# Output projection as seven block products over two query groups, shared products added by VectorE from its banks; first statistics spread by TensorE

## The reference

```python
xn = (x - mean(x)) / sqrt(var(x) + 1e-5)                    # per token
q, k, v = split(xn @ Wqkv + bqkv)                           # one head, d = 512
attn = softmax(q @ k.T / sqrt(512)) @ v                     # 2048 x 2048 per sequence
gate = softmax over the 16 largest of 64 (xn @ Wq_w.T @ keys.T), 0 elsewhere
z = (xn @ A_w.T).reshape(.., 64, 8) * gate                  # 512 columns
out = x + attn @ Wo + bo + (z @ B_w.T) * 2
```

## Time and profile before

| | |
|---|---|
| median of 3 runs | 2846.6 us (2846.41 to 2846.97) |
| profiled execution, its own time | 2843.56 us |
| its span | 2841.0 us |
| TensorE, VectorE, ScalarE, GpSimd busy | 97%, 53%, 30%, 14% of the span |
| matmuls in the trace | 12096 |
| mean over the 16 DMA engines | 224 GB/s |

### The profile page before, as it was taken

The page is one execution under the profiler, slowest core; times in us unless marked ns, Lnnn a source line. Parts: engine busy times, 40 slices in busy tenths (PEclk is TensorE's granted clock), DMA queues, the critical chain, the costliest instruction groups (busy, mean ns, idle before and its releaser), DMA issues.

```text
span 2841.0 us, 33300 instructions
## 1 busy us (share of the span) xinstructions
PE 2749.1 (97%) x12096; PEld 2244.6 (79%) x12096; DVE 1496.1 (53%) x1875; ACT 854.7 (30%) x1146; POOL 389.6 (14%) x293
## 2 busy tenths in 40 slices
PE   6888999999999999999979999999999999999999
PEld 4676878878888888888868788888888888888887
DVE  6665876467745776455574634324444344333431
ACT  3552225622364233322242221111322212112110
POOL 0011000000000000000031504205032050320501
PEclk9999999999999999999989999999999999999999
DMA  7589665455555364324766967758688686775866
GB/s 299 184 300 319 218 209 199 148 163 178 174 200 157 119 216 138 97 97 163 253 244 247 343 226 253 279 203 296 240 275 303 238 287 216 250 281 197 284 233 234
DMA packets 268159, 636.01 MB, mean 224 GB/s; under 512 B 30192, under 2 KB 54896, under 8 KB 263792
## 3 DMA queue, kind: packets, MB, share of 16 engines
q1 hardware_dynamic: 233968, 546.54, 56.2%
...
## 4 chain that ended last, share of the span: by engine, by line
PE 85%; DVE 5%; DMA 4%; ACT 3%; issue 2%; SPq 0%; POOL 0%; ACTq 0%; DVEq 0%; POOLq 0%
PE psum L750 35%; PE psum L1632 15%; PE psum L1634 15%; PE psum L1633 15%; PE psum L687 2%; DMA stat_scratch<-mv 2%; DMA w_raw<-t_scratch 1%; ACT rows L534 1%; DVE prob L1834 1%; DMA w_raw<-W_blocks 1%; DVE r_lo L1806 1%; ACT w_hi L479 1%; DVE w_lo L800 1%; ACT rows L537 1%; PE psum L1755 0%
## 5 line engine op out<-in xcount | busy, mean ns | idle before, releaser
L800 DVE TENSOR_TENSOR w_lo<-w_raw,w_hi 128x1024 fp32r<-128x1024 f32 x224 | 274.2, 1224 | 433.7 <-ACT w_hi L479 433.5
L479 ACT ACTIVATE w_hi<-w_raw 128x1024 fp32r<-128x1024 f32 x224 | 237.5, 1060 | 775.2 <-PE psum L750 677.8
L1632 PE MATMUL psum<-r_hi,f_hi 128*128 128x512 f32 x1024 | 401.9, 392 | 4.6 <-DVE r_lo L1806 3.3
L1634 PE MATMUL psum<-r_hi,f_lo 128*128 128x512 f32 x1024 | 399.2, 390 | 0.0
L1633 PE MATMUL psum<-r_lo,f_hi 128*128 128x512 f32 x1024 | 399.1, 390 | 0.0
L750 PE MATMUL psum<-s_hi,w_hi 128*128 128x512 f32 x896 | 353.7, 395 | 28.1 <-DVE w_lo L800 16.4
L750 PE MATMUL psum<-w_hi,s_hi 128*128 128x512 f32 x896 | 351.4, 392 | 15.9 <-DVE w_lo L800 14.9
L750 PE MATMUL psum<-s_hi,w_lo 128*128 128x512 f32 x896 | 351.3, 392 | 0.0
L750 PE MATMUL psum<-s_lo,w_hi 128*128 128x512 f32 x896 | 351.3, 392 | 0.0
L750 PE MATMUL psum<-w_lo,s_hi 128*128 128x512 f32 x896 | 350.3, 391 | 0.0
L750 PE MATMUL psum<-w_hi,s_lo 128*128 128x512 f32 x896 | 350.2, 391 | 0.0
...
## 6 DMA issues: line engine op xcount, KB each, us to landing
...
w_raw<-t_scratch SPq DMA_DIRECT2D x128, 512.0 KB, 4.0
...
res<-x SPq DMA_DIRECT2D x128, 256.0 KB, 6.1
out<-res SPq DMA_DIRECT2D x128, 256.0 KB, 7.2
...
```

The costliest lines, as they stand in the source:

```text
L479: nc.scalar.activation(w_hi[:, s % RAW], w_raw[:, s % RAW], ACT.Copy).then_inc(s_whi, 1)
L800: nc.vector.tensor_tensor(w_lo[:, s % RAW], w_raw[:, s % RAW], w_hi[:, s % RAW].bitcast(F32), ALU.subtract).then_inc(s_wlo, 1)
L1632: pe.matmul(bank, sh, mh, start=first, stop=False)
L1634: return pe.matmul(bank, sl, mh, start=False, stop=last)
```

## The change

**Output projection.** Two query groups (1024 tokens, rows 1 and 2) and two column halves of 1024 form 2 x 2 blocks: x11, x21 are attn of the two groups, x12, x22 their z; b11, b12 are the halves of Wo, b21, b22 of B_T. An output stage w covers a pair (w // 2) and 512 columns of each half (w % 2), and takes seven products of 512 tokens x 512 columns with an inner size of 512, two items each: 14 items, 336 matmuls. Sums of x blocks (s1 to s4, `sum_x`) and their low parts (`low_x`) are made by VectorE, 128x1024 each; high parts by ScalarE. Sums of weight blocks (t1 to t4) are made once by GpSimd beside S0 to V1 (`sum_weights`, 16 of 128x1024, with 16 loads and 16 stores of 0.5 MB) and kept in `sum_scratch`. A finished product is added from its banks to the one to three quarters of the output that need it (`take_product`, 40 additions a stage), except that products 2, 3 and 6 go on accumulating in a bank of an earlier one (CHAINED). The accumulators `part_out` hold x plus bias; GpSimd's queue loads x in 1 MB quarters (`load_rows`), SP stores quarters of 1 MB (`store`).

Since a pair must be complete first, the order of stages is now S0 S1 V0 V1, then S t, O t-2, V t for t = 2 to 7, then O6 O7, written out without loops. Weights are split in O0 and O1 now. A product's addition trails its last item: two tiles in each of the next two items, and the last product's eight additions stand at the start of the next value stage. The low part of z and attn is made where it is used (`low_x`), not in the value stage.

**First statistics.** For group 0 the second half is spread by TensorE too, behind item 6 of the first product (`spread_own`), without DRAM. VectorE computes two of its four tiles (bn_stats), ScalarE the other two; the rows are loaded early into buffers that are free then. x12's rows come as one transfer of 2 MB by GpSimd's queue, the sums of the second product (MIX0) begin one item earlier, and VectorE takes the first part of product 1's result (`take_first_kq`) instead of ScalarE.

```diff
+MIX0_AT = [(0, 7), (1, 0), (1, 1), (1, 2), (1, 3), (1, 4), (1, 5), (1, 6), (1, 7)]
...
-OWN_AT = {(0, 3): 4, (0, 5): 6, (0, 6): 7}
+OWN_AT = {(0, 0): 4, (0, 2): 6}
...
+    def own_rows(j):
+        source = (rows[:, 1, :], part[:, 1, 0:4, :].rearrange("p a c -> p (a c)"),
+                  part[:, 1, 4:8, :].rearrange("p a c -> p (a c)"), part[:, 2, 0:4, :].rearrange("p a c -> p (a c)"))
+        return source[j - HT]
...
+                    if first and (idx, s) == (0, 7):
+                        for a in range(2):
+                            act.wait_ge(s_spread, 3 + a)
+                            nc.scalar.activation(mean_rstd[:, a, W:TG], psum[:, a, :], ACT.Copy).then_inc(s_stat0, 1)
...
+                    if static(g) and g == 0 and (idx, s) == (0, 6):
+                        spread_own()
...
+        def spread_own():
+            for a in range(2):
+                bank_read(pe, 0, 0, 0, a)
+                pe.wait_ge(s_diag, HT + 2 + a)
+                for j in range(HT):
+                    mm = pe.matmul(psum[:, a, j * P:(j + 1) * P], ones[:],
+                                   part[:, 2, HT + a, j * P:(j + 1) * P], start=True, stop=True)
+                mm.then_inc(s_spread, 1)
...
+            elif block == 1 and static(g) and g == 0:
+                dve.wait_ge(s_x12, 16)
...
+        def take_first_kq(banks):
...
+                nc.vector.scalar_tensor_tensor(part[:, 1, b, :], psum[:, b, :], b_diff[:, b:b + 1],
+                                               part[:, 0, b, :], ALU.add, ALU.add).then_inc(s_evA, 1)
...
-                        if s == 4:
-                            stats_of_tile(HT + 1)
+                        if s in (3, 4):
+                            stats_of_tile(HT + 1 + 2 * (s - 3))
...
+                            rstd_finish(2, (HT + 2) * TILE_STEPS + RSTD_STEPS, slice(HT, NTOK))
+                            dve.wait_ge(s_rstd, 2)
+                            for a in range(2):
+                                nc.vector.tensor_tensor(
+                                    part[:, 2, HT + a, :].rearrange("p (a b) -> p a b", b=P),
+                                    ident[:].unsqueeze(1).to_broadcast([P, HT, P]),
+                                    mv[:, a, HT:NTOK].unsqueeze(2).to_broadcast([P, HT, P]), ALU.mult).then_inc(s_diag, 1)
+                    if first and (idx, s) in MIX0_AT:
+                        step = MIX0_AT.index((idx, s))
...
+        pool.wait_ge(s_tiles, 2)
+        pool.dma_start(xb[:, 1], xT[HK * P:2 * HK * P, 0:W].rearrange("(a p) t -> p a t", p=P)).then_inc(s_x12, 16)
...
+    PRODUCTS = [("x11", "b11"), ("s3", "t3"), ("x12", "b21"), ("x22", "t4"), ("s2", "t2"), ("s4", "b22"), ("s1", "t1")]
+    CHAINED = (2, 3, 6)
...
+    EV = {0: 0, 1: 12, 2: 16, 3: 20, 4: 24, 5: 28, 6: 32}
+    EVS = 40
+    X_SUMS = {"x11": 0, "x12": 0, "x22": 0, "s1": 1, "s2": 2, "s3": 1, "s4": 3}
...
+    STAGES = [("S", 0), ("S", 1), ("V", 0), ("V", 1)]
+    for t in range(2, NQ):
+        STAGES += [("S", t), ("O", t - 2), ("V", t)]
+    STAGES += [("O", NQ - 2), ("O", NQ - 1)]
...
+                if kind == "O":
+                    sp.wait_ge(b_qlo, 2 * (t + 3))
...
+                    if PRODUCTS[i // 2][1][0] == "t":
+                        sp.wait_ge(b_wst, 16 * 16)
...
+        def store(w, c):
+            base, col = out_rows(w, c)
+            sp.wait_ge(b_oev, w * EVS + {C11: EV[3], C21: EV[5], C12: EVS, C22: EVS}[c])
+            sp.dma_start(out[base:base + QG, col:col + W].rearrange("(j p) w -> p j w", p=P),
+                         out_quarter(w, c)).then_inc(b_st[c], 16)
...
+                if i == 10:
+                    store(w, C11)
...
+                        mm = three(psum[:, P_BANK[q][j], :], xh[:, a, tok], xl[:, a, tok], wh[:, cols], wl[:, cols],
+                                   begin and q not in CHAINED, end)
...
+            else:
+                pe.wait_ge(b_oev, (t - 2) * EVS + EV[5] + d + 1)
...
+            b11, b12, b21, b22 = (weight_piece(n) for n in ("b11", "b12", "b21", "b22"))
...
+            pool.wait_ge(b_wld, 16 * 4 * (kt + 1))
+            nc.gpsimd.tensor_tensor(b12, b22, b12, ALU.subtract).then_inc(b_wsum, 1)
+            pool.wait_ge(b_wsum, 4 * kt + 1)
+            nc.gpsimd.tensor_tensor(b11, b12, b11, ALU.add).then_inc(b_wsum, 1)
+            pool.wait_ge(b_wsum, 4 * kt + 2)
+            nc.gpsimd.tensor_tensor(b21, b21, b11, ALU.subtract).then_inc(b_wsum, 1)
+            nc.gpsimd.tensor_tensor(b22, b22, b11, ALU.subtract).then_inc(b_wsum, 1)
...
+        def load_rows(w, c):
...
+            pool.dma_start(out_quarter(w, c),
+                           x[base:base + QG, col:col + W].rearrange("(j p) w -> p j w", p=P)).then_inc(b_x, 16)
...
+            elif t == 1:
...
+            else:
+                for c in (C22, C21, C12, C11):
+                    load_rows(t - 2, c)
+                for c in (C22, C21, C12, C11):
+                    add_bias(t - 2, c)
...
+            if t < NQ:
+                sums(t, range(1, 10))
...
+        def sum_x(w, j):
...
+            if name == "s3":
+                nc.vector.tensor_tensor(low, x11, x21, ALU.subtract).then_inc(b_xsum, 1)
...
+            nc.vector.tensor_tensor(low, x21, x22, ALU.add).then_inc(b_xsum, 1)
+            if steps >= 2:
+                dve.wait_ge(b_xsum, base + 1)
+                nc.vector.tensor_tensor(low, low, x11, ALU.subtract).then_inc(b_xsum, 1)
...
+                dve.wait_ge(b_xsum, base + 2)
+                nc.vector.tensor_tensor(low, x12, low, ALU.subtract).then_inc(b_xsum, 1)
...
+        def low_x(w, j):
...
+            nc.vector.tensor_tensor(lo, source, hi.bitcast(F32), ALU.subtract).then_inc(b_xlo, 1)
...
+        def take_product(w, q, tiles):
...
+            for j in tiles:
+                product_ready(dve, w, q, j)
+                if q == 0:
+                    for c in (C22, C21, C12):
+                        dve.wait_ge(b_xb, 4 * QT * w + (BIAS_ORDER[w].index(c) + 1) * QT)
+                        add_product(w, c, j, BANK_A[j])
...
+                    add_product(w, C12, j, BANK_B[j])
+                else:
+                    dve.wait_ge(b_oev, base + EV[5] + j + 1)
+                    add_product(w, C12, j, BANK_A[j])
+                    add_product(w, C22, j, BANK_A[j])
...
+        def output(w):
+            t = w + 2
+            for i in range(LEN["O"]):
+                split_next("O", w, i)
...
+                if i >= 2 and i // 2 - 1 < NP - 1:
+                    take_product(w, i // 2 - 1, (0, 1) if i % 2 == 0 else (2, 3))
...
+                if i + 2 < LEN["O"]:
+                    low_x(w, i + 2)
...
+                if t < NQ and 3 <= i <= 7:
+                    less_maximum(t, 2 * i - 6)
+                    less_maximum(t, 2 * i - 5)
+                if i + 3 < LEN["O"]:
+                    sum_x(w, i + 3)
...
+                if t < NQ and i == LEN["O"] - 1:
+                    low_probability(t, 0)
+                    low_probability(t, 1)
...
+                if t >= 2 and i == 0:
+                    take_product(t - 2, NP - 1, range(QT))
...
+                if i <= 2 and t != 1:
+                    less_maximum(t, 10 + 2 * i)
+                    less_maximum(t, 11 + 2 * i)
...
+        stages({"S": scores, "O": output, "V": values})
+        take_product(NQ - 1, NP - 1, range(QT))
```

1326 lines of the change are left out of this document (792 added, 534 removed).

## The result

| | before | changed |
|---|---|---|
| median of 15 runs each | 2845.08 us (2839.83 to 2847.81) | 2850.04 us (2845.17 to 2857.05) |
| ratio, 95% interval | | 1.002 (1.0012 to 1.0029) |
| profiled execution, its span | 2843.56, 2841.0 us | 2847.05, 2845.2 us |

A second measurement on another chip gave 1.0023 (1.0013 to 1.0033). So the change costs 0.1 to 0.3%, though it removes 384 matmuls.

What follows compares the result with a forecast made beforehand. TensorE's matmuls (97% of the span) were taken as the bound. -87.2 - 21 + 30 + 6 + 26 + 16 + 3 + 12 + 8 = -7 on 2843.6 us gave 2836.4, as a median 2839; range 2792 to 2886.

Steps and rivals of the forecast that it cites:

- the start of phase B: Stages S0, V0, S1, V1: 209 us instead of 204.5, and 7 for sharing with GpSimd; +12, ends -5 and +35.
- the sharing: VectorE instructions with two SBUF inputs beside GpSimd additions: about 1.0 us of VectorE per GpSimd addition.
- First statistics: Phase A's second block product: 50 us instead of 67.8, with 3 in the next; -21, ends -10 and -26.
- Removed matmuls: Output stages: 384 matmuls fewer at 227 ns each, 87.2 us less.
- O0 and O1: Output stages 0 and 1, which also split the weights: VectorE has more work than TensorE; +26, ends +14 and +44.
- the tail: Behind the last matmul: eight additions and 2 MB of stores, 12.2 us against 3.7; +8, ends 5 and 12.
- O2 to O5: Output stages 2 to 5: a wait of 4.2 us each at item 10, ends 0 and 9 per stage; +16.
- R2: Rival: sharing with GpSimd costs next to nothing, output stages 2 to 5 lose nothing; 2794 us, faster, chance 0.25.
- Value stages: Second item of six value stages: TensorE waits 5 us each for p_lo, range 3.2 to 6.1; +30.
- The clock: TensorE's lower clock behind the new waits, 0 to 1.5 us each: +6, ends 0 and 15.
- R3: Rival: some 24 MB of transfers in S0 and S1, 16.5 fit, 20 us late; 2859 us, chance 0.15.
- R1: Rival: VectorE becomes the bound; output stages 2 to 5 lose 9, 0 and 1 lose 25; 2883 us, chance 0.20.

Runs made afterwards that it cites:

- the separate run: The kernel before with phase A of the changed kernel, so the spread of the first statistics alone: 2834.83 us, ratio 0.9946 to the kernel before.
- The first experiment on it: The changed kernel with the last product's eight additions behind the low parts of a value stage's items 1, 2 and 3: ratio 1.0044 to the kernel before.

## Why the prediction was wrong

- **The step that failed** is "the start of phase B", "+12, ends -5 and +35": +29. It is inside the stated ends, but alone it turns the sign. Its stage values add to 205.6 and not to the 209 written, a slip of 3.4. Measured against them: "S0 and S1 come to about 45.3 each" took 102.1 instead of 90.6 (without the wait for V0), V0 with the wait before it 73 instead of 59, V1 58.3 instead of 56; together 27.9 more, for which 7 of sharing had been set aside.
- **In S0 and S1 it is the keys.** TensorE stood 8.0 us in four waits and ran behind them at the lower clock. The step allowed 1.7 for each stage, "transposes or a first wait". The kernel before has one wait of this kind in S0, 1.7 us; the others there are the chain of maxima and subtractions ahead of V0. TensorE's waits from S0 to V0 before, then in S0 and at the first matmul of S1 after:

```profile
PE psum L1632 <- issue: 4.7, 1, 4.7
PE psum L1676 <- DVE diag L1829: 1.7, 1, 1.7
PE psum L1632 <- DVE r_lo L1806: 1.7, 1, 1.7
PE psum L1670 <- DVE run_max L1821: 1.5, 1, 1.5
...
PE psum L1801 <- DVE r_lo L2120: 5.0, 3, 3.5
PE psum L1801 <- issue: 3.0, 1, 3.0
```

The last one is S1's first item: its r_lo, read back from `split_scratch`, was issued at 1408.78 and took 8.5 us to land, and the matmul started at 1417.36. The DMA engines were busy 0.99 of the time to 1420, and from 1363.14 to 1417.3 they moved 4.19 MB for GpSimd's queue, the first quarter of the weights and its sums, which the kernel before doesn't move there. The kernel with fewer transfers keeps just this quarter and has the waits too (8.1 us). So whether this quarter makes the keys late was not tested. With the first statistics alone the wait is 1.6 us, so phase A isn't the cause.
- **Before V0 it is the sharing**: "7 more for the sharing with GpSimd's 16 weight additions" became 10.4 us by the kernel without them, 8.5 of it in one wait. The only price in the prediction is that of the earlier trace rows, per GpSimd addition of 128x512; here they are 128x1024 and stand in fours on the chain to V0. But even without these additions S0 to V1 takes 223.1 us, 17.5 over the stage values, and 14.8 of that is S0 and S1 (their key waits are 12.0 us in that run). The sharing was 3.4 us too low; the keys were the larger error.
- **The sharing was taken as a rate.** "About 1.0 us of VectorE per GpSimd addition" holds for 128x512 (1.6 to 1.8 instead of 0.68). The mechanism is turns by whole instructions, so the price is the length of GpSimd's instruction: 2.1 us for each of 128x1024. The Trainium skill (SBUF — State Buffer, Who interferes with whom) says so: only the pair of ports that the two share causes contention, and it is an exclusive lock. The runs here agree: 2.7 to 2.9 us beside instructions of 128x1024 and 1.6 to 1.8 beside 128x512, for a VectorE instruction that takes 0.68 alone.
- **First statistics**, the second term that failed: -21 against -13 by the profile and -14.7 by the separate run (the border moves by up to 13 us from profile to profile, so the second is the better number). The wait of 13.38 us is gone as forecast and the second product takes 52.1 us where 50 was forecast. The "3 in the next" did not come: behind the second product 3.05 us of wait remain, against 4.06. In all, group 0 takes 358.3 instead of 374.5 us; phase A also begins its matmuls 0.9 us later, and its other three groups take 1.8 more.
- **Removed matmuls, O0 and O1, the tail**: right. 77.54 us for a dense output stage (76 + 2 forecast), +22 for +26, +7 for +8.
- **O2 to O5**: forecast 4.2 us each with the wait at item 10; O3, O4 and O5 have none. An addition from PSUM takes 0.69 us in the record, but six of them in a row take 3.67, 0.61 each; and GpSimd's nine sums in O3 held five of VectorE's SBUF instructions for 1.0 us each, 5.0 in all where 6.6 were assumed. So R2's outcome came in these stages, without its reason: the sharing is there, the backlog just doesn't reach TensorE.
- **Value stages**: a wait of 2.4 to 5.9 us at the second item, ended by p_lo: right in mechanism, place and size (+37 against 30 and the clock's share). V3 alone takes 59.1 us against 48.0 when dense, and 2.4 us of that are two waits for transfers of r_lo, which were not forecast. The first experiment on it shows that moving the additions removes it, and that the queues behind decide whether this is worth anything.
- **The clock** was charged 6 us. From matmul starts (0.40 to 0.52 us apart instead of 0.227) phase B spends 31 us more than at full clock in the changed kernel and 7 before. About 8 us lie in O0 and O1 and 10 in V2 to V7, so in part they are inside the terms above. A wait of 3 us was enough: V2, V6 and V7 were granted 0.97 with it, V5 1.00. In O0 waits of 3.2, 1.8 and 2.9 us were each followed by matmuls at the lower level, 22 in all. The reading of the earlier trace rows, that 4.1 us of idle time leave the clock alone, was one case, of two waits of 0.7 and 3.3 us. The same trace has another, a single wait of 4.06 us that ends at 150.38, and behind it the clock was 0.50:

```profile
150.38:155.60 5.22, 5.22 (x12) 4.14 (x13) 5.12 (x5) 1.74 (x3) 0.00 (x0) 0.50 0.11 43
```

- **The rivals**: R3 named score stage 1 waiting for r_lo from its transfer, and S1's first matmul did wait for it, 3.0 us. Its size was 20 us; S0 and S1 took 11.5 over the forecast. The later 12 of the weights' 16 MB are not at fault (S0 and S1 take 99.4 instead of 102.1 us without them), the first 4 may be. R1 didn't come: O3 to O5 are dense.
- **The number.** The start of phase B (17 over) and phase A (8 over) missed in one direction, the output stages (12 under, mostly O2 to O5) in the other. That the time came out only 11 us from the forecast is in part luck.
